# Fewer and longer runs of small products on TensorE, in a delta-rule attention block with a feed-forward part

## The chip, the cores and the metric

The kernel runs on one core of one Trainium2 chip. The metric is the device time of one execution in microseconds (us). The engines are named as in the profile: PE is TensorE (PEld its weight loads), DVE is VectorE, ACT is ScalarE, POOL is GpSimd, SP is SyncE.

## The reference

The input is `hidden_states` of shape [2, 4096, 512] in float32. It is normalized per token (`xn`), and the output is the input plus two branches of `xn`:

```python
q, k = hidden @ Wq, hidden @ Wk            # 16 heads of 32; both divided by their length
v = silu(hidden @ Wv); beta = sigmoid(hidden @ Wb)
# per head, token by token:
v_pred = S^T k_t
delta  = (v_t - v_pred) * beta_t
S      = S + k_t delta^T
o_t    = S^T q_t
attn   = (o * rsqrt(mean(o*o) + eps) * o_norm_weight) @ Wo
ffn    = (silu(xn @ gate_w8 * gate_scale) * (xn @ up_w8 * up_scale)) @ down_w8 * down_scale
out    = x + attn + ffn
```

The feed-forward weights (512 to 1536 and back) are first rounded to float8_e4m3.

## The kernel before, in words

The sequence is cut into 16 turns of 256 tokens of each of the two batches, 512 tokens a turn. In each turn the recurrence over 32 tokens at a time is put into matrix form. There are 64 heads-and-pieces on each quarter of 32 partitions (four heads lie on the four quarters), in eight groups of eight.

PE's program of a turn is written out by hand, and every step of it waits on semaphores of the engines that feed it:

- **Projections** (`project`, 13 jobs of 12 matmuls of 128x512, job 4 of 8): queries, keys, values and beta, each into one of the four banks `D`. Keys are jobs 0, 2, 5, 7, queries 1, 3, 6, 8, beta 4, values 9 to 12. ACT copies keys and queries into `kq` (`evacuate_k`, `evacuate_q`), and a job may write its bank once the job four earlier has been read.
- **Products of keys with keys and queries** (`gram(g)`, groups 0 to 7): 64 float32 products on 32x32 tiles each, into the four banks `T`. Groups 4 to 7 use the banks of 0 to 3 again, after DVE has read them (`read_grams(0)`, `mask_products(0)`). They stand between the projections.
- **Output projection** of the turn before (`project_out`, 4 jobs of 12) and the first 20 of 24 **feed-forward halves** (`gate_up(half)`, 8 matmuls each). Meanwhile DVE inverts the triangular matrices by row elimination (`row_products`, `off_rows`, 31 pairs), and between the rows it reads values (`v_to_tokens`), adds the output (`add_out`) and multiplies gate and up (`fuse_tile`). At the end it transposes the inverse in two halves (`t_transposed`).
- **Products with the inverse** (groups 0 to 7, 64 small products each, line 525): groups 0 to 3 wait for the first transposed half, groups 4 to 7 for the second and for the bank to be read by DVE (`read_w(g)`) and ACT (`copy_u(g)`). The last four feed-forward halves stand between them, half of one (4 matmuls) behind each group.
- **The chain** of eight steps: per step 64 small products with the state, six matmuls of the down projection (line 502), 64 small products that update the state, six more. It starts when all eight `read_w` and `copy_u` are done. The next turn's normalization and transposes are in it too.

The small products all go through `quads`, four 32x32 products on the four diagonal tiles, line 350 in the profile. At the head of a turn DVE runs `prepare`: it normalizes the outputs of the turn before (`o_sums`, `o_scale`, which frees ACT to make `o_hi`, then `o_low`), transposes keys (`k_to_tokens`) and beta, and reads the first products. In the opening turn `prepare_first` stands in its place, with the rounding of weights.

SP's queue carries two loads and two stores a turn; the order of its program depends on `add_out` alone.

Of the kernel before, what the change touches and what calls it, by code (L numbers as in the profile page):

```python
# [20 lines left out]
IC = INNER // P  # L21
# [5 lines left out]
PROJECTIONS = 13  # L27
# [20 lines left out]
LOW_BEFORE, LATE_HALVES = 8, 4  # L48
# [13 lines left out]
def gate_up_job(half):  # L62

    return JOB_GU + half


def bank_of(job):

    return job % 4 if job < JOB_DN + 3 else JOB_DN % 4
# [24 lines left out]
def delta_block_kernel(nc: bass.Bass, x: bass.AP, wq: bass.AP, wk: bass.AP, wv: bass.AP, wb: bass.AP,  # L94
# [11 lines left out]
    with ctx:  # L106
# [238 lines left out]
        def _(pe):  # L345
# [36 lines left out]
            def all_spans(it=0):  # L382
                for turn in range(TURNS):
# [33 lines left out]
                    def project(job, first=0, end=12):  # L417
                        bank = bank_of(job) if first else take(job)
                        group = (4, 0, 5, 1, 12, 6, 2, 7, 3, 8, 9, 10, 11)[job]
                        cols = slice(group * P, (group + 1) * P)  # L420
                        parts = ((w_hi, xt_hi), (w_hi, xt_lo), (w_lo, xt_hi))[:2 if job == JOB_B else 3]
                        products = [(k, w, xp) for k in range(KT_) for w, xp in parts]
                        for n in range(first, min(end, len(products))):
                            k, w, xp = products[n]
                            last = nc.tensor.matmul(D[bank][:, :], w[:, k, cols], xp[:, k, :],  # L425
                                                    start=n == 0, stop=n == len(products) - 1)
                        if n == len(products) - 1:
                            last.then_inc(dense_done, 1 + TILES if opening and job == JOB_V[MS - 1] else 1)

                    def gate_up(half, first=0, end=KT_):  # L430
                        bank = bank_of(gate_up_job(half)) if first else take(gate_up_job(half))
                        ic, side = divmod(half, 2)
                        c = side * INNER + ic * P
                        for k in range(first, end):
                            nc.tensor.matmul(D[bank][:, :], wgu[:, k, c:c + P], xt_hi[:, k, :], start=k == 0, stop=False)  # L435
                            last = nc.tensor.matmul(D[bank][:, :], wgu[:, k, c:c + P], xt_lo[:, k, :],  # L436
                                                    start=False, stop=k == KT_ - 1)
                        if end == KT_:
                            last.then_inc(dense_done, 1)

                    def gram(g):

                        pe.wait_ge(kwide_ready, since(MS, g // 2 + 1))
                        pe.wait_ge(qwide_ready, since(MS, g // 2 + 1))

                        if g < 4:
                            pe.wait_ge(o_ready, since(STEPS))
                        else:
                            pe.wait_ge(m_ready, since(2, 1))
                            pe.wait_ge(p_ready, since(2, 1))  # L450
                        pe.nop(nofuse=True)
                        for n in range(8):
                            both = kq_flat.rearrange("p (n t) -> p n t", t=2 * CHUNK)[:, 8 * g + n, :]
                            last = quads(T[g % 4][:, 64 * n:64 * n + 64], both[:, 0:CHUNK], both)
                        last.then_inc(tiled_done, 1)
# [2 lines left out]
                    pe.wait_ge(xt_lo_ready, since(TILES, TILES))  # L458
                    for job in range(5):
                        project(job)  # L460
                    gram(0)
                    gram(1)
                    project(5)
                    gram(2)
                    gram(3)
                    project(6)
                    project(7)
                    project(8)
                    gram(4)
                    gram(5)  # L470
                    project(9, end=5)
                    gram(6)
                    gram(7)
                    project(9, first=5)
                    for job in range(10, PROJECTIONS):
                        project(job)

                    if opening:
# [36 lines left out]
                    for g in range(8):  # L515
                        pe.wait_ge(tt_ready, since(2, g // 4 + 1))
                        if g < 4:
                            pe.wait_ge(m_ready, since(2, 2))
                            pe.wait_ge(p_ready, since(2, 2))
                        else:  # L520
                            pe.wait_ge(u_ready, since(8, g - 3))
                        pe.nop(nofuse=True)
                        for n in range(8):
                            pc = 8 * g + n
                            last = quads(T[g % 4][:, 64 * n:64 * n + 64], tt[:, pc // 32, :, pc % 32], kpv[:, 1:3, pc * DH:(pc + 1) * DH])
                        last.then_inc(tiled_done, 1)
                        gate_up(2 * IC - LATE_HALVES + g // 2, 2 * (g % 2), 2 * (g % 2) + 2)

                    def transpose_next(j):

# [4 lines left out]
                    for c in range(STEPS):  # L535
# [25 lines left out]
                        fill(fill_at(c, 1))  # L561

            all_spans()


# [6 lines left out]
        def _(act):  # L572
# [21 lines left out]
            def all_spans(it=0):  # L594
                for turn in range(TURNS):
# [13 lines left out]
                    def evacuate_k(m):  # L609
                        full(("job", JOB_K[m]))  # L610
                        bank = bank_of(JOB_K[m])
                        nc.scalar.activation(kq[:, m * BC:(m + 1) * BC, 0, :], D[bank][:, :].rearrange("p (n t) -> p n t", t=CHUNK),
                                             ACT.Copy).then_inc(kwide_ready, 1)

                    def evacuate_q(m):
                        full(("job", JOB_Q[m]))
                        bank = bank_of(JOB_Q[m])
                        nc.scalar.activation(kq[:, m * BC:(m + 1) * BC, 1, :], D[bank][:, :].rearrange("p (n t) -> p n t", t=CHUNK),
                                             ACT.Copy).then_inc(qwide_ready, 1)
# [9 lines left out]
                    evacuate_q(0)  # L629
                    evacuate_k(1)  # L630
                    evacuate_q(1)
                    evacuate_k(2)
                    if not opening:
                        act.wait_ge(on_ready, since(1))
                        nc.scalar.activation(o_hi, o_normed.rearrange("p (m n) -> p m n", m=MS), ACT.Copy).then_inc(ohi_ready, 1)
                    def beta_tanh():

                        act.wait_ge(b_summed, since(1, 1))
                        nc.scalar.activation(tb[:, :, :], tb[:, :, :], ACT.Tanh, scale=w_inv[:, 3:4]).then_inc(tb_ready, 1)

                    if not opening:
                        beta_tanh()
                    evacuate_q(2)
                    evacuate_k(3)
                    evacuate_q(3)
# [191 lines left out]
        def _(dve):  # L837
# [129 lines left out]
            def all_spans(it=0):  # L967
                for turn in range(TURNS):
# [25 lines left out]
                    def k_to_tokens(m):  # L994
                        dve.wait_ge(kwide_ready, since(MS, m + 1))
                        nc.vector.transpose(kt[:, m * BC:(m + 1) * BC, :], kq[:, m * BC:(m + 1) * BC, 0, :]).then_inc(kt_ready, 1)
# [63 lines left out]
                    def times_beta(s):  # L1060

                        dve.wait_ge(beta_ready, since(2, s + 1))
                        solved[0] = step(nc.vector.tensor_tensor(m_prob[:, s], m_prob[:, s],
                                                                 beta_t[:, s].unsqueeze(1).to_broadcast([P, CHUNK, CHUNK]), ALU.mult))
# [8 lines left out]
                    def prepare():  # L1073

                        o_sums(it, turn, after, step)
                        k_to_tokens(0)
                        k_to_tokens(1)
                        o_scale(it, turn, after, step)
                        b_to_tokens()
                        k_to_tokens(2)  # L1080
                        read_grams(0)
                        mask_products(0)
                        o_low()
                        beta_to_problems()
                        beta_over_k(0)
                        times_beta(0)
                        k_to_tokens(3)
                        set_diagonal(0)

# [36 lines left out]
                    def low_part(ic):  # L1126
                        dve.wait_ge(fhi_ready, since(IC, ic + 1))
                        nc.vector.tensor_tensor(f_lo[:, ic, :], fuse[:, ic % FUSE_RING, :], f_hi[:, ic, :],
                                                ALU.subtract).then_inc(flo_ready, 1)
# [89 lines left out]
                    low_part(8)  # L1219
                    read_w(1)  # L1220
                    low_part(9)
                    read_w(2)
                    read_statistics(0)
                    read_w(3)
                    fuse_tile(10)
                    read_w(4)
                    read_statistics(1)
                    read_w(5)
                    aggregate(0)
                    low_part(10)  # L1230
                    read_w(6)
                    aggregate(1)
# [106 lines left out]
```

## Time and profile before

| what | value |
|---|---|
| time, median of 3 runs | 2445.73 us (2445.45 to 2448.61) |
| profiled execution, its own time | 2442.38 us |
| its span, first to last instruction | 2440.6 us |
| PE busy | 95% of the span, 40944 matmuls |
| DVE busy | 74% |
| ACT busy | 35% |
| POOL busy | 11% |
| mean granted clock of TensorE | 0.992 |
| one steady turn, start to start | about 144.7 us |

PE is busy nearly all the time, so idle time of the others costs nothing unless PE waits for it. "Issue" is time in which an engine waited for nothing that the profile shows; a wait for a semaphore whose signal can't be paired can stand under that name too.

### The profile page before, as it was taken

The numbers are of one execution on the slowest core, as the hardware profiler recorded it, in microseconds if no ns is written. First come the engines' busy times: TensorE is split into PE (matmuls) and PEld (weight loads), VectorE is DVE, ScalarE is ACT, GpSimd is POOL, SyncE is SP. The second block draws the span as 40 slices with busy tenths as digits, with TensorE's granted clock in tenths as the row PEclk, the third lists the DMA queues.
The fourth block names the chain that finished last, engine by engine and source line by source line (L and its number), as shares of the span: only waits on it lengthen the run. The fifth ranks groups of instructions, "written<-read, shape, count | busy, mean of one in ns | idle before, by whom it ended". The sixth has DMA issues, their size and how long they took to land.

```text
span 2440.6 us, 90080 instructions
## 1 busy us (share of the span) xinstructions
PE 2314.6 (95%) x40944; PEld 1259.3 (52%) x40944; DVE 1817.7 (74%) x3210; ACT 861.2 (35%) x2069; POOL 275.0 (11%) x521
## 2 busy tenths in 40 slices
PE   1869999999999999999999999999999999999996
PEld 0435555554655545455554555555465554545553
DVE  7985866869677695867769586686967769586785
ACT  2353432524234252423425243242423425242341
POOL 3011002010010101001010110201001010100100
PEclk9989999999999999999999999999999999999999
DMA  6100100100010010100001010010101001010000
GB/s 216 48 1 4 36 3 3 36 3 36 4 36 3 3 36 3 36 3 12 27 3 36 3 36 3 3 36 3 36 4 36 3 3 36 3 36 3 11 28 19
DMA packets 27163, 54.30 MB, mean 22 GB/s; under 512 B 5152, under 2 KB 5152, under 8 KB 26784
## 3 DMA queue, kind: packets, MB, share of 16 engines
q1 hardware_dynamic: 26784, 48.55, 5.7%
q8 instruction: 323, 5.29, 0.9%
q14 instruction: 56, 0.46, 0.1%
HBM read 31.76 MB, written 16.78 MB: 20 GB/s over the span
## 4 chain that ended last, share of the span: by engine, by line
PE 93%; DVE 4%; issue 1%; SPq 1%; DMA 0%; POOL 0%; ACT 0%; POOLq 0%; DVEq 0%
PE T L350 22%; PE D L425 21%; PE D L502 15%; PE D L435 14%; PE D L436 13%; PE D L366 7%; PE D L355 1%; DMA ds_row<-in_L_ffn_down_scale_dram 0%; DVE wd L267 0%; DVE wgu L267 0%; DVE w_lo L921 0%; DVE outer_v L1145 0%; DVE at L1152 0%; SPq L300 0%; SPq L295 0%
## 5 line engine op out<-in xcount | busy, mean ns | idle before, releaser
L435 PE MATMUL D<-xt_hi,wgu 128*128 128x512 f16 x1536 | 586.3, 382 | 18.5 <-ACT sg L674 12.1
L436 PE MATMUL D<-xt_lo,wgu 128*128 128x512 f16 x1536 | 584.7, 381 | 0.0
L425 PE MATMUL D<-xt_hi,w_hi 128*128 128x512 f16 x832 | 317.1, 381 | 38.5 <-DVE wo_lo L925 38.5
L425 PE MATMUL D<-xt_lo,w_hi 128*128 128x512 f16 x832 | 316.5, 380 | 0.0
L502 PE MATMUL D<-wd,f_hi 128*128 128x512 bf16 x768 | 293.6, 382 | 0.3 <-issue 0.3
L425 PE MATMUL D<-xt_hi,w_lo 128*128 128x512 f16 x768 | 292.3, 381 | 0.0
L502 PE MATMUL D<-wd,f_lo 128*128 128x512 bf16 x768 | 291.1, 379 | 0.0
L1152 DVE TENSOR_TENSOR at<-at,outer_v 128x62 f32<-128x62 f32 (+15 forms) x496 | 262.4, 529 | 12.8
L1145 DVE TENSOR_TENSOR outer_v<-mt,at 128x62 f32<-128x62 f32 (+15 forms) x496 | 260.7, 526 | 11.7
L435 PEld LDWEIGHTS D<-xt_hi,wgu 128*128 128x128 f16 x1536 | 150.5, 98 | 195.7 <-ACT sg L674 12.6
L436 PEld LDWEIGHTS D<-xt_lo,wgu 128*128 128x128 f16 x1536 | 150.9, 98 | 167.4 <-issue 2.8
L664 ACT ACTIVATE kpv<-kpv,rk 128x32 f32<-128x32 f32 x1024 | 230.9, 306 | 11.0 <-POOL rk L813 9.6
L674 ACT ACTIVATE sg<-D,gs 128x512 f32<-128x512 f32 x192 | 131.8, 687 | 174.1 <-PE D L436 171.8
L668 ACT ACTIVATE f_hi<-fuse 128x512 f16<-128x512 f32 x192 | 120.6, 628 | 167.2 <-DVE fuse L1138 166.9
L350 PEld LDWEIGHTS T<-kpv,mt 32*32 32x32 f32 x8192 | 131.0, 134 | 72.6 <-issue 72.6
L350 PE MATMUL T<-kpv,mt 32*32 32x64 f32 x8192 | 148.2, 219 | 17.5 <-issue 17.5
L1264 DVE STREAM_TRANSPOSE outer_p<-T 128x256 f32<-128x256 f32 x128 | 57.6, 450 | 137.8 <-PE T L350 137.8
L1246 DVE STREAM_TRANSPOSE outer_v<-T 128x256 f32<-128x256 f32 x128 | 57.6, 450 | 131.7 <-PE T L350 131.7
L350 PEld LDWEIGHTS T<-kq,state 32*32 32x32 f32 x8192 | 121.4, 105 | 61.8 <-issue 61.5
L829 POOL TENSOR_TENSOR xs<-xs,fuse 128x512 f32<-128x512 f32 x64 | 81.1, 1267 | 639.5 <-DVE fuse L1240 639.5
L719 ACT ACTIVATE qt<-T 128x256 f32<-128x256 f32 x128 | 49.1, 383 | 291.3 <-DVE outer_p L1264 291.3
L425 PEld LDWEIGHTS D<-xt_hi,w_hi 128*128 128x128 f16 x832 | 81.5, 98 | 134.5 <-DVE wo_lo L925 38.9
(169 smaller groups left out, 3207.4 us busy)
## 6 DMA issues: line engine op xcount, KB each, us to landing
xs<-_attn_hidden_states_dram SPq DMA_DIRECT2D x34, 512.0 KB, 3.4
out_dram<-xs SPq DMA_DIRECT2D x32, 512.0 KB, 3.1
f_hi<-in_L_ffn_down_w_dram SPq DMA_DIRECT2D x2, 768.0 KB, 6.8
f_lo<-in_L_ffn_down_w_dram SPq DMA_DIRECT2D x2, 768.0 KB, 8.3
qt<-in_L_ffn_gate_w_dram SPq DMA_DIRECT2D x2, 768.0 KB, 4.3
kpv<-in_L_ffn_up_w_dram SPq DMA_DIRECT2D x2, 768.0 KB, 4.3
qt<-in_L_attn_Wq_dram SPq DMA_DIRECT2D x1, 1024.0 KB, 10.2
kpv<-in_L_attn_Wk_dram SPq DMA_DIRECT2D x1, 1024.0 KB, 13.1
```

Of the source, the lines that this page charges most:

```text
L350: last = nc.tensor.matmul(out[s], lhs[s], rhs[s], start=start, stop=True, skip_group_check=shared)
L366: ins = nc.tensor.matmul(D[bank][:, :], o_part[:, m, j * P:(j + 1) * P], w[:, m, :], start=n == 0, stop=n == 11)
L425: last = nc.tensor.matmul(D[bank][:, :], w[:, k, cols], xp[:, k, :], start=n == 0, stop=n == len(products) - 1)
L435: nc.tensor.matmul(D[bank][:, :], wgu[:, k, c:c + P], xt_hi[:, k, :], start=k == 0, stop=False)
L436: last = nc.tensor.matmul(D[bank][:, :], wgu[:, k, c:c + P], xt_lo[:, k, :], start=False, stop=k == KT_ - 1)
L502: last = nc.tensor.matmul(D[bank][:, :], (f_hi, f_lo)[n % 2][:, ic, j * P:(j + 1) * P], wd[:, ic, :], start=n == 0, stop=n == 2 * IC - 1)
L664: return nc.scalar.activation(v_problem, v_problem, ACT.Identity, scale=rk[:, n:n + 1])
L668: nc.scalar.activation(f_hi[:, ic, :], fuse[:, ic % FUSE_RING, :], ACT.Copy).then_inc(fhi_ready, 1)
L674: nc.scalar.activation(sg[:, ic % 2, :], D[bank_of(gate_up_job(2 * ic))][:, :], ACT.Silu, scale=gs[:, ic:ic + 1]).then_inc(sg_ready, 1)
L829: nc.gpsimd.tensor_tensor(xs[:, par, j, :], xs[:, par, j, :], fuse[:, j % 2, :], ALU.add).then_inc(acc_ready, 1)
L1145: solved[0] = step(nc.vector.tensor_tensor(products(j), m_prob[:, :, j, j + 1:].unsqueeze(3).to_broadcast(shape), t_prob[:, :, j, 0:j + 1] ...
L1152: solved[0] = step(nc.vector.tensor_tensor(rest, rest, products(j), ALU.subtract))
```

## The change

In PE's program the eight groups of products of keys and queries stand in two runs of four, with four whole projections between them; before they stood in four runs of two, the last of them in the middle of job 9. The eight groups of products with the inverse stand in four runs of two, with one whole feed-forward half behind each; before each group had half of one behind it. On ACT the copy of the third key job moves behind `o_hi` and beta; on DVE its transpose moves behind `times_beta(0)`, and the statistics of the next turn's input move forward by one or two reads. The number of instructions is the same.

```diff
@@ PE
                     for job in range(5):
                         project(job)
-                    gram(0)
-                    gram(1)
-                    project(5)
-                    gram(2)
-                    gram(3)
-                    project(6)
-                    project(7)
-                    project(8)
-                    gram(4)
-                    gram(5)
-                    project(9, end=5)
-                    gram(6)
-                    gram(7)
-                    project(9, first=5)
-                    for job in range(10, PROJECTIONS):
+                    for g in range(4):
+                        gram(g)
+                    for job in range(5, 9):
+                        project(job)
+                    for g in range(4, 8):
+                        gram(g)
+                    for job in range(9, PROJECTIONS):
                         project(job)
...
                         last.then_inc(tiled_done, 1)
-                        gate_up(2 * IC - LATE_HALVES + g // 2, 2 * (g % 2), 2 * (g % 2) + 2)
+                        if g % 2:
+                            gate_up(2 * IC - LATE_HALVES + g // 2)
@@ ACT
                     evacuate_q(1)
-                    evacuate_k(2)
                     if not opening:
                         act.wait_ge(on_ready, since(1))
                         nc.scalar.activation(o_hi, ...).then_inc(ohi_ready, 1)
...
                     if not opening:
                         beta_tanh()
+                    evacuate_k(2)
                     evacuate_q(2)
@@ DVE, prepare
                         b_to_tokens()
-                        k_to_tokens(2)
                         read_grams(0)
                         mask_products(0)
                         o_low()
                         beta_to_problems()
                         beta_over_k(0)
                         times_beta(0)
+                        k_to_tokens(2)
                         k_to_tokens(3)
@@ DVE, behind the inverse
                     low_part(9)
+                    read_statistics(0)
                     read_w(2)
-                    read_statistics(0)
                     read_w(3)
+                    read_statistics(1)
                     fuse_tile(10)
                     read_w(4)
-                    read_statistics(1)
+                    aggregate(0)
                     read_w(5)
-                    aggregate(0)
                     low_part(10)
```

## Rows read from the trace of the kernel before

**Rows 1.** The page: PE's busy time, and the chain that ended last
```profile
PE 2314.6 (95%) x40944; PEld 1259.3 (52%) x40944; DVE 1817.7 (74%) x3210; ACT 861.2 (35%) x2069; POOL 275.0 (11%) x521
...
PE 93%; DVE 4%; issue 1%; SPq 1%; DMA 0%; POOL 0%; ACT 0%; POOLq 0%; DVEq 0%
```

**Rows 2.** Windows: length, busy PE, PEld, DVE, ACT, POOL, clock, DMA, GB/s
```profile
1262.00:1282.00 20.00, 20.00 (x569) 12.41 (x567) 13.30 (x17) 4.42 (x6) 1.80 (x1) 1.00 0.01 3
1282.00:1336.00 54.00, 54.00 (x251) 24.36 (x249) 52.28 (x97) 28.97 (x87) 3.92 (x13) 1.00 0.12 40
1336.00:1354.00 18.00, 16.80 (x553) 10.78 (x556) 11.65 (x25) 5.48 (x12) 1.78 (x2) 1.00 0.02 5
```

**Rows 3.** Waits of PE: us in total, times, longest
```profile
PE T L350 <- issue: 20.8, 28, 1.6
```

**Rows 4.** Timeline of PE, projections and chain: start, length, instruction, count
```profile
1257.74 0.38 PE L425 MATMUL D<-xt_hi,w_lo 128*128 128x512 f16 x1
...
1279.61 0.38 PE L425 MATMUL D<-xt_lo,w_hi 128*128 128x512 f16 x1
1279.92 2.00 PE L350 MATMUL T<-kq 32*32 32x64 f32 x128
1281.85 0.39 PE L425 MATMUL D<-xt_hi,w_lo 128*128 128x512 f16 x1
...
1285.74 0.38 PE L425 MATMUL D<-xt_hi,w_lo 128*128 128x512 f16 x1
...
1356.01 0.38 PE L502 MATMUL D<-wd,f_lo 128*128 128x512 bf16 x1
1356.32 1.10 PE L350 MATMUL T<-kpv 32*32 32x64 f32 x64
1357.35 0.39 PE L502 MATMUL D<-wd,f_hi 128*128 128x512 bf16 x1
```

**Rows 5.** Timeline of PE at the products with the inverse
```profile
1335.82 0.38 PE L436 MATMUL D<-xt_lo,wgu 128*128 128x512 f16 x1
1337.17 1.15 PE L350 MATMUL T<-kpv,mt 32*32 32x64 f32 x64 [0.98 <-issue]
...
1351.55 1.15 PE L350 MATMUL T<-kpv,mt 32*32 32x64 f32 x64
...
1353.29 0.38 PE L436 MATMUL D<-xt_lo,wgu 128*128 128x512 f16 x1
1353.90 1.09 PE L350 MATMUL T<-kq,state 32*32 32x64 f32 x64 [0.22 <-ACT kpv L679]
```

**Rows 6.** Timeline of DVE from `prepare` to the transposed inverse
```profile
1277.36 0.70 DVE L996 STREAM_TRANSPOSE kpv<-kq 128x512 f32<-128x512 f32 x1
1277.99 0.17 DVE L1027 TENSOR_TENSOR at<-sig_t,rkk_t 128x32 f32<-128x32 f32 x1
1281.98 1.25 DVE L1053 STREAM_TRANSPOSE mt<-T 128x1024 f32<-128x1024 f32 x1 [3.81 <-PE T L350]
...
1286.81 0.71 DVE L1000 STREAM_TRANSPOSE kpv<-D 128x512 f32<-128x512 f32 x1
...
1334.23 0.74 DVE L1138 SCALAR_TENSOR_TENSOR fuse<-D,usf,sg 128x512 f32<-128x512 f32 x1
...
1335.72 2.37 DVE L1162 STREAM_TRANSPOSE mt<-at 128x1024 f32<-128x1024 f32 x2
```

**Rows 7.** Timeline of ACT: a key job's copy, and the last copy_u
```profile
1258.16 0.60 ACT L612 ACTIVATE kq<-D 128x512 f32<-128x512 f32 x1 [1.99 <-PE D L425]
...
1353.26 0.38 ACT L679 ACTIVATE kpv<-T 128x256 f32<-128x256 f32 x1 [1.68 <-DVE kq L1167]
```

**Rows 8.** Timeline of PE in the opening turn
```profile
185.15 1.15 PE L350 MATMUL T<-kpv,mt 32*32 32x64 f32 x64 [1.54 <-issue]
```

**Rows 9.** Instruction fetches of the page, and a gap on PE's timeline
```profile
q8 instruction: 323, 5.29, 0.9%
...
1489.37 0.34 PE L350 MATMUL T<-kpv,mt 32*32 32x64 f32 x6 [0.43 <-issue]
```

**Rows 10.** Windows, a stretch of the opening turn; columns as in rows 2
```profile
108.50:118.70 10.20, 5.63 (x79) 3.34 (x80) 9.82 (x12) 10.17 (x11) 0.00 (x0) 0.50 0.04 4
```

## The prediction, made before the kernel was run

> **What bounds the kernel now.** I read the page first, then PE's waits, a table of stages for one steady turn (the ninth of sixteen), and last the timelines of PE, DVE and ACT there. PE is busy for 95% of the span and is 93% of the chain that ended last [rows 1]. So the time is the sum of PE's work and of its few waits; what other engines do counts only where PE waits for them. In the three stages of the turn PE is full in the first two and short by 1.2 us of 18 in the third, where the inverse is handed over [rows 2]. DVE, though, is busy for 52.28 of 54.00 us in the stage of the row elimination [rows 2]: there it is a second chain, nearly as tight as PE's. PE's waits in the steady part are two in each turn: about 0.9 to 1.0 us, shown as "issue", ahead of the first product with the inverse, and 0.22 ahead of the first product with the state; the others are rare gaps or belong to the opening and the end [rows 3, 5].
>
> The first wait is DVE's: its transposes of the inverse begin at 1335.72 and the two take 2.37, so the first ends near 1336.9, and PE starts at 1337.17 [rows 5, 6]. Without it PE would have started 0.31 behind the matmul at 1335.82, as behind any dense matmul ahead of a small run [rows 4], at 1336.13. The wait is worth 1.04 us.
>
> **What a switch costs.** Dense matmuls follow each other every 0.216 us (18 steps between 1281.85 and 1285.74) [rows 4]. From the last dense matmul to the next one, a run of 128 small products takes 2.24 us (1279.61 to 1281.85), one of 64 takes 1.34 (1356.01 to 1357.35) [rows 4]. So 64 small products cost 0.90, and of the 1.34 there remain 1.34 - 0.216 - 0.90 = 0.22, plus about 0.01 by which the first dense step is longer: 0.23 us for going from dense to small and back. For products with the inverse the period of one run and four dense matmuls is (1351.55 - 1337.17) / 7 = 2.054 us [rows 5]; less 4 x 0.216 and 0.90 that leaves 0.29. Their own pace may be a little slower than 0.90 for 64, so I take 0.28; the bounds are 0.23 and 0.29.
>
> **The change, part by part.**
> *Keys and queries.* Four runs of two become two of four: two switches fewer, 0.46 us. The last run also loses what stood ahead of it: five of the twelve matmuls of project(9), 5 x 0.216 = 1.08 us, now follow. The last of these products is therefore ready 0.46 + 1.08 = 1.54 us earlier in the turn. DVE had been idle for 3.81 us waiting for it [rows 6], so read_grams(1) and the elimination move up too, if DVE's earlier work is done. It is: in the new order the products of groups 0 to 3 end before project(5) rather than after it, and the last thing DVE needs, k_to_tokens(3), gets its data from job 7. Behind job 7 PE still has project(8), 2.59 us, and four groups, 3.6; less 0.42 until ACT starts and 0.60 of its copy [rows 4, 7] that is 5.2 us ahead, for two DVE operations of 0.70 and 0.17 [rows 6]. Moving k_to_tokens(2) and evacuate_k(2) costs nothing: both engines are idle around them, and the copy o_hi, which o_low waits for, is now ahead of job 5's evacuation, which couldn't start before project(5) ended anyway. If that cover were gone, each would cost up to 0.7 us.
>
> But DVE can't move by the whole 1.54. Its second value transpose needs job 10. That job's last matmul starts at 1285.74 and its data can be read 0.42 later, as ACT started at 1258.16 behind the matmul at 1257.74 [rows 4, 7]: at 1286.16. DVE came at 1286.81 [rows 6], 0.65 late. Now PE's job 10 moves up by 0.46 only, to 1285.70, and DVE comes at 1286.81 - 1.54 = 1285.27: a new stall of 0.43 us. The elimination then ends 1.54 - 0.43 = 1.11 us earlier. The later reads of PE's banks in the elimination had more to spare. The least has fuse_tile(8), at 1334.23 [rows 6]: its job ended 16 steps of 0.216 ahead of 1335.82, so it could be read from 1332.8 on, 1.4 us earlier. Of that 0.65 goes, so there is no second stall. PE arrives 0.46 earlier. So the wait shrinks to 1.04 + 0.46 - 1.11 = 0.39, and this part gives **1.11 us** a turn: 0.46 of switches and 0.65 of wait. Bounds: 0 (if DVE gains nothing, the switches saved only lengthen the wait) and 1.50 (both whole).
>
> *Products with the inverse.* Eight runs become four: 4 x 0.28 = 1.12 us. What is late next? Group 4 needs copy_u(0), 5 needs copy_u(1), and so on. A pair now takes 2.05 + 0.90 + 0.86 = 3.83 us, so group 4 starts at 7.7 us of the stage and group 7 at 12.4; copy_u(0) to (3) are done by about 2.5, 3.4, 5.9 and 6.7, worked out from DVE's 0.45 and ACT's 0.38 behind each group's last product. The end gains: before, PE waited for copy_u(7), which started at 1353.26, 1.71 behind its group's start at 1351.55 [rows 5, 7]. The chain started at 1353.90, 0.61 behind the last dense matmul at 1353.29, where 0.31 is normal: 0.30 lost. Now eight dense matmuls, 1.73 us, stand behind group 7 in place of four, which covers copy_u(7) with about 0.6 to spare. So this part gives 1.12 + 0.30 = **1.42 us**. The reordered statistics and aggregates lie in DVE's gaps; they are ready earlier, and POOL idles until they come.
>
> *Sum.* 1.11 + 1.42 = 2.53 us in each of 15 turns, 38.0. In the opening turn the first stage is held by other waits of DVE and ACT, and the second group of four inverses starts at 185.15 behind a wait of 1.54 [rows 8]; from there two switches and the last wait go, 0.86 us. In all 38.8. The profiled execution took 2442.38 us for its span of 2440.6, so it would be 2403.6; the median of the runs shown is 3.35 above it, which gives 2445.73 - 38.8 = **2406.9 us**.
>
> **The rivals.**
> *The inverse ends no sooner.* DVE is full in that stage [rows 2], and a further read that comes late, or slower elimination steps, could hold it. Against: its start waited on PE with 3.81 us idle. Then only 15 x 1.42 + 0.86 = 22.2 are won: 2423.6.
> *The switch isn't saved.* If the 0.23 were a cost of the first and last products that waiting instructions between groups inside a run also bring, only the moved work counts: 0.65 + 0.30, 14.5 us in all, 2431.2. Against: 128 products in one run with such a wait in the middle cost only 0.90 more than 64 [rows 4].
> *The longer runs starve for instructions.* One fetched block of 5.29 MB / 323 = 16 KB serves some 127 products with their loads, and the only gaps inside small runs are named issue, as 0.43 at 1489.37 [rows 9]. A run of four uses two blocks in 3.6 us. A gap of 0.43 in each of the two runs takes 15 x 2 x 0.43 = 13 us back: 2420. Against: of PE's gaps named issue there are 28 in all [rows 3], over half of them the wait for the inverse, and 448 small runs. [...]
> *TensorE's clock falls: slower.* The opening has whole stretches at half clock, one of 10.20 us at 0.50, when PE was busy for 5.63 of it with narrow products [rows 10]. If a run of four small groups, 3.6 us with little of the array at work, did the same, a stretch in which PE is otherwise full loses half of 10.2, 5.1 us. One such stretch in each of 15 turns costs 76.5, less 38.8: 2483. It decides from eight stretches on. Against: in the stage of the eight runs, half of it such products, the clock stayed at 1.00 [rows 2]. [...]
>
> **How the numbers follow.** The forecast 0.66; the inverse no sooner 0.12; starved runs 0.07; switch not saved 0.04; some other stall in either stage, which would give 2410 to 2425, 0.04; clock 0.04; another loss or none 0.03. Measurement tells apart about 0.2%, 5 us. Faster 0.93, same 0.02, slower 0.05. The lower end is both parts whole, 15 x (1.50 + 1.42) + 0.86 = 44.7: 2401. The upper end is the rival in which the inverse ends no sooner, 2424. Between them lie some 0.85.
>
> **What would show it.** The page: PE's instructions unchanged, its waits of "issue" ahead of the inverse near 0.3 rather than 0.95; no wait on ACT L679 in the steady turns. Timeline: two runs of 256 small products of some 3.7 us, four of 128 with the next run 3.83 later; DVE's second L1000 of a turn with an idle of about 0.4 ahead of it; a turn 2.5 us shorter. Wrong if gaps stand inside the long runs, if the granted clock falls below 1.00 in steady turns, or if the wait ahead of the inverse grows to 1.5.

## The result, and the profile after

The change makes the kernel slightly slower: 2452.26 us median of 20 runs (2445.0 to 2457.17) against 2444.68 of 20 runs of the kernel before (2439.2 to 2448.61), ratio 1.0032, interval 1.0025 to 1.0038. I had forecast 2406.9, in a range of 2401 to 2424. The profiled execution took 2453.12 us, its span 2451.4 (before 2440.6).

The page after, as in [rows 1] (busy time, then the chain that ended last):

```profile
PE 2301.0 (94%) x40944; PEld 1265.2 (52%) x40944; DVE 1817.1 (74%) x3210; ACT 853.8 (35%) x2069; POOL 268.6 (11%) x521
...
PE 92%; DVE 4%; issue 2%; SPq 1%; DMA 0%; POOL 0%; ACT 0%; POOLq 0%; DVEq 0%
```

PE does the same 40944 matmuls in less busy time, and yet the span is 10.8 us longer: PE waits more. Its waits say under which name, as in [rows 3] (us in total, times, longest):

```profile
PE T L350 <- issue: 50.5, 54, 2.1
```

That is 30 us more of "issue" ahead of small products, and the wait for ACT's copy is gone from the list. The windows of the same turn, as in [rows 2], say where:

```profile
1266.00:1288.00 22.00, 19.33 (x565) 12.37 (x564) 13.76 (x16) 4.54 (x6) 1.80 (x1) 1.00 0.01 3
1288.00:1343.00 55.00, 55.00 (x258) 24.96 (x256) 52.82 (x97) 28.35 (x87) 3.93 (x13) 1.00 0.11 39
1343.00:1361.00 18.00, 16.72 (x590) 11.37 (x592) 11.23 (x25) 5.49 (x12) 1.41 (x2) 1.00 0.02 5
```

The stage of keys and queries, full before, now lacks 2.7 us of PE, at a clock of 1.00. And PE's timeline there (rows for small runs alone; a run that is broken by a gap has two rows) shows the gaps inside the runs:

```profile
1266.95 3.14 PE L350 MATMUL T<-kq 32*32 32x64 f32 x209
1271.44 0.87 PE L350 MATMUL T<-kq 32*32 32x64 f32 x47 [1.35 <-issue]
1282.71 2.44 PE L350 MATMUL T<-kq 32*32 32x64 f32 x158
1286.46 1.61 PE L350 MATMUL T<-kq 32*32 32x64 f32 x98 [1.32 <-issue]
1343.71 2.09 PE L350 MATMUL T<-kpv,mt 32*32 32x64 f32 x128 [0.29 <-issue]
1347.57 2.10 PE L350 MATMUL T<-kpv,mt 32*32 32x64 f32 x128
1351.43 2.08 PE L350 MATMUL T<-kpv,mt 32*32 32x64 f32 x128
1355.27 2.08 PE L350 MATMUL T<-kpv,mt 32*32 32x64 f32 x126
1358.34 0.27 PE L350 MATMUL T<-kpv,mt 32*32 32x64 f32 x2 [0.99 <-issue]
1360.37 1.09 PE L350 MATMUL T<-kq,state 32*32 32x64 f32 x64
```

In this turn a gap stands neither between groups (a group is 64 products) nor at a wait: 209 + 47 and 158 + 98 break in the middle of the fourth group and of the third. The 15 steady turns hold such a gap of 1 to 2 us in 26 of their 30 runs of four groups, and in a few runs of two.

The other steps of the forecast are there. The wait ahead of the inverse is 0.29 in place of 0.98 [rows 5]. Two of the runs above follow each other in 3.86 us. DVE had 6.04 us of idle time ahead of its read, and its second value transpose has the new stall (DVE's timeline, to be held against [rows 6]):

```profile
1288.11 1.25 DVE L1046 STREAM_TRANSPOSE mt<-T 128x1024 f32<-128x1024 f32 x1 [6.04 <-PE T L350]
...
1293.39 0.72 DVE L993 STREAM_TRANSPOSE kpv<-D 128x512 f32<-128x512 f32 x1 [0.35 <-PE D L425]
```

**Where the gaps stand.** I numbered PE's recorded instructions (weight loads, matmuls, semaphore events) from the first on, and took all distances of over 0.25 us between the starts of two neighbouring small products of the 15 steady turns. Beside them are the records of the queue that fetches PE's instructions, in packets of 16384 bytes, 323 of them after for 82729 recorded instructions. The table is worked out from the records of three traces that lack none of PE's:

```
kernel   gaps  with number mod 256     sum of    from the end of the last fetched
               = 192 or 193            the gaps  packet to the next product, min/median/max
before    17    17                      7.8 us   1.25 / 1.41 / 1.57
after     41    41                     51.7 us   1.20 / 1.40 / 1.73
e5        42    42                     52.0 us   1.20 / 1.40 / 1.57
```

Every gap of over 0.25 us, before and after, stands where a block of 256 instructions ends, and ends 1.4 us after the packet with the next block has landed. The seven other traces of the experiments below say the same: 233 more gaps, all with the number 192 or 193 (four of these traces lack 256 records of dense matmuls, and there the small products were counted by their weight loads). A packet of 16384 bytes for 256 instructions is 64 bytes for each. I read this as PE having run out of instructions. For the gap that ends at 1271.44 the packet began 2.7 us and ended 1.5 us ahead of the product; the block ahead of it, which ends 209 products into the run, had been used up in 1.8 us.

The theory for the experiments, an estimate from these records: PE has the block that it works through and one more at hand. With boundaries and packets numbered from the first on, 830 of the 983 packets of the three traces began behind the boundary of their own number (0.9 to 1.05 us behind it in the median), the other 153 up to 4.8 us ahead of it, none ahead of the boundary before that, and every gap ends behind the packet with the number of the boundary before it. So the fetch of a further block mostly begins when a block is done, and that block can be used some 3.3 us later (2.9 to 4.0 in the runs of four that have a gap: 0.6 to 1.6 us to the packet, 0.9 to 1.5 for it, about 1.4 behind it). A block of dense matmuls lasts 27 us (27.4 to 27.6 in the steady turns of before and after), and in e5 the 58 boundaries among dense matmuls of the steady turns are passed at the usual step of 0.216 us. One of small products alone lasts 128 x 0.014 = 1.8 us, so it leaves a gap of 1.4 to 1.9 us at its end. Rivals: an order of work that makes somebody late (waits for copies, DVE's preparation), longer runs that are slow by themselves, and the clock.

### The profile page after: what moved, and what is told of

It reads as the page before. It is cut to its first block, busy times and chain, and to the rows that moved or that the text cites. A ratio compares the mean times of both kernels' runs of the same rounds, so it can differ in the third digit from the quotient of the medians.

```text
span 2451.4 us, 90080 instructions
## 1 busy us (share of the span) xinstructions
PE 2301.0 (94%) x40944; PEld 1265.2 (52%) x40944; DVE 1817.1 (74%) x3210; ACT 853.8 (35%) x2069; POOL 268.6 (11%) x521
## 4 chain that ended last, share of the span: by engine, by line
PE 92%; DVE 4%; issue 2%; SPq 1%; DMA 0%; POOL 0%; ACT 0%; POOLq 0%; DVEq 0%
PE T L350 21%; PE D L425 21%; PE D L494 15%; PE D L435 14%; PE D L436 13%; PE D L366 7%; PE D L355 1%; DMA ds_row<-in_L_ffn_down_scale_dram 0%; DVE wd L267 0%; DVE wgu L267 0%; DVE w_lo L914 0%; DVE outer_v L1138 0%; DVE at L1145 0%; SPq L295 0%; SPq L300 0%
## 5 line engine op out<-in xcount | busy, mean ns | idle before, releaser
L1145 DVE TENSOR_TENSOR at<-at,outer_v 128x62 f32<-128x62 f32 (+15 forms) x496 | 263.2, 531 | 12.8
L350 PE MATMUL T<-kq 32*32 32x64 f32 x8192 | 129.0, 215 | 37.6 <-issue 37.6
```

The costliest lines, as they stand in the source:

```text
L350: last = nc.tensor.matmul(out[s], lhs[s], rhs[s], start=start, stop=True, skip_group_check=shared)
L1145: solved[0] = step(nc.vector.tensor_tensor(rest, rest, products(j), ALU.subtract))
```

## The experiments

All ratios are to the kernel before, run on the same chip.

### e1 and e2: each part alone

e1 is the kernel before with the part of the inverse alone:

```diff
-                        gate_up(2 * IC - LATE_HALVES + g // 2, 2 * (g % 2), 2 * (g % 2) + 2)
+                        if g % 2:
+                            gate_up(2 * IC - LATE_HALVES + g // 2)
```

with the moved statistics of DVE. e2 has the part of keys and queries alone, with the moved copy and transpose:

```diff
-                    gram(0)
-                    gram(1)
-                    project(5)
-                    gram(2)
...
+                    for g in range(4):
+                        gram(g)
+                    for job in range(5, 9):
+                        project(job)
+                    for g in range(4, 8):
+                        gram(g)
```

> The kernel before with the inverse part of the change alone: four runs of two groups, a whole feed-forward half behind each, and DVE's statistics moved. Theory (instruction blocks): PE's program is fetched in blocks of 256 instructions of which only the next one is on its way, and PE stops where a block of nearly only small products is used up in 1.8 us, before the next is there some 3.3 us after the last change of blocks. A run of two groups is 258 instructions, so it holds a whole block only where a block begins within a dozen instructions of the run's start: gaps in some four turns of fifteen, about 5 us in all. The switches and the last wait give 22 us: 17 us faster than before, ratio 0.993. Rival (the longer runs of products with the inverse are slow by themselves, by waits for copies): no gain or a loss, ratio 1.000 or more, with a gap in every turn at the same group.

> The kernel before with the keys-and-queries part alone: two runs of four groups, and the moved copy and transpose. Theory (instruction blocks): each run of 520 instructions holds at least one whole block, so each has a gap of 1.2 to 2 us in every turn, some 45 us in 15 turns, against 1.11 x 15 = 17 us won: about 25 us slower, ratio 1.010. Rival (order of the work, a wait of DVE's preparation or of the copies): the loss would stand in front of groups, not inside them, and DVE's first read of groups 4 to 7 would find its own work late; here it should find 4 us or more of idle time. Rival (clock): granted clock below 1.00 in steady turns, gaps absent.

e1: 2437.51 us, ratio 0.9955 (0.9942 to 0.9968). e2: 2467.57 us, ratio 1.0076 (1.0063 to 1.0089). So the first part wins 9 to 11 us and the second loses 19 to 21; together they give the small loss of the whole. The expectation had the signs and the order (17 won, 25 lost), and both parts were 4 to 8 us off. e2's timeline has the same picture in the same places, at the same number of products into the run as the whole change, with 5.78 us of idle time for DVE ahead of its read of groups 4 to 7, so DVE's own work isn't late:

```profile
1275.07 3.14 PE L350 MATMUL T<-kq 32*32 32x64 f32 x209
1279.38 0.87 PE L350 MATMUL T<-kq 32*32 32x64 f32 x47 [1.16 <-issue]
1290.64 2.50 PE L350 MATMUL T<-kq 32*32 32x64 f32 x158
1294.13 1.61 PE L350 MATMUL T<-kq 32*32 32x64 f32 x98 [0.98 <-issue]
```

e1 has a gap of over 0.25 us inside a run of two in four of 60 runs, two to four products ahead of its end, where a block began with the run:

```profile
1478.93 2.09 PE L350 MATMUL T<-kpv,mt 32*32 32x64 f32 x128 [0.78 <-issue]
1482.89 2.08 PE L350 MATMUL T<-kpv,mt 32*32 32x64 f32 x126
1486.61 0.27 PE L350 MATMUL T<-kpv,mt 32*32 32x64 f32 x2 [1.64 <-issue]
1488.64 2.13 PE L350 MATMUL T<-kpv,mt 32*32 32x64 f32 x128
```

These four come to 5.6 us, as expected. What I had left out are the small ones: distances of over 0.13 us between neighbouring small products, less 0.035 us each, came to 20 us in all, against 9.5 in the kernel before. More than half of them, of 0.2 to 0.9, lie in the chain of eight steps, though its program is that of before.

### e3 and e4: the same work, the blocks in two places

A turn of PE's program has 5156 instructions, 36 more than 20 blocks, so the boundaries wander by 36 from turn to turn. To hold them still, e3 adds to e1 waits that are always fulfilled, each one instruction:

```diff
+            for _ in range(10):
+                pe.wait_ge(consts, 2)
+                pe.nop(nofuse=True)
             pe.wait_ge(proj_ready, 5)
...
                     for half in range(2 * IC - LATE_HALVES):
                         gate_up(half)
+                        for _ in range(11):
+                            pe.wait_ge(consts, 2)
+                            pe.nop(nofuse=True)
```

e4 is e3 with 122 in place of 10.

> The kernel of e1 with 220 waits that are always fulfilled added to PE's program in each turn, 11 behind each of the first 20 feed-forward halves, and 10 ahead of the first turn. Each turn is then 5376 = 21 x 256 instructions, so that the block boundaries fall at the same places in each turn, 76 to 190 instructions into each small run outside the chain, away from the starts. Theory (instruction blocks): no gap of over 0.4 us in any steady turn; about 5 to 8 us faster than e1, 22 to 27 faster than before, ratio 0.990, if waits between dense matmuls cost nothing. Rival (gaps come at random or from other engines): as many gaps as e1, and the same time or longer by the added instructions.

> As e3, and only the number of fulfilled waits ahead of the first turn differs: 122 in place of 10. Work, order and instructions of every turn are the same. Now a block begins exactly with the first run of products with the inverse. Theory (instruction blocks): one gap of 1.2 to 1.6 us near the end of that first run in each of 15 turns, some 20 us slower than e3, ratio to before about 0.998. Rival (anything that lies in the work or its order): the same time as e3 within 0.1%.

e3: 2424.74 us, ratio 0.9916 (0.9903 to 0.9929). e4: 2466.0 us, ratio 1.0084 (1.0068 to 1.01). The two differ in the number of waits ahead of the first turn, in a place where PE is idle for 38 us anyway, and in nothing else, and by 41 us. e3 is 13 us faster than e1 (5 to 8 were expected) though it issues 3530 instructions more, and its longest distance between two small products inside a run is 0.59 us. PE's timeline of the same turn in e3:

```profile
1038.01 2.09 PE L350 MATMUL T<-kpv,mt 32*32 32x64 f32 x128 [0.93 <-issue]
1041.86 2.13 PE L350 MATMUL T<-kpv,mt 32*32 32x64 f32 x128
1045.76 2.08 PE L350 MATMUL T<-kpv,mt 32*32 32x64 f32 x128
1049.60 2.08 PE L350 MATMUL T<-kpv,mt 32*32 32x64 f32 x128
1053.44 1.10 PE L350 MATMUL T<-kq,state 32*32 32x64 f32 x64
```

and in e4:

```profile
1050.69 2.08 PE L350 MATMUL T<-kpv,mt 32*32 32x64 f32 x127 [0.95 <-issue]
1054.41 0.21 PE L350 MATMUL T<-kpv,mt 32*32 32x64 f32 x1 [1.64 <-issue]
1056.39 2.13 PE L350 MATMUL T<-kpv,mt 32*32 32x64 f32 x128
```

The gap stands where it was forecast, in each of the 15 turns, and is 1.6 to 2.1 us from start to start, more than the 1.4 of the theory's arithmetic. The size of the whole was off by a factor of two: some 20 us were expected, 41 were measured. In the profiled executions the gaps over 0.13 us come to 43.5 us in e4 and 7.4 in e3, 36 of the 44 us between their spans; the boundaries behind the first run fall badly in other places too. Part of the rest is the clock: in two turns, right behind the two longest gaps of the steady turns (2.13 us), the granted clock was 0.50 for 3.4 us while PE did dense matmuls, one every 0.43 us (columns as in [rows 2]):

```profile
1201.30:1204.70 3.40, 3.40 (x9) 1.04 (x8) 2.22 (x4) 0.38 (x1) 0.00 (x0) 0.50 0.02 5
```

The rivals that look to the work or its order are out.

### e5, e6, e7: the runs of four, and the kernel before, with the blocks held still

The same waits added to the changed kernel (e5 with 20 ahead of the first turn, e6 with 200) and to the kernel before (e7, with 10).

> The changed kernel with the 220 fulfilled waits of e3 in each turn, and 20 ahead of the first, so that block boundaries stand still: 180 and 76 instructions into the two runs of four groups, 48 to 102 into the runs with the inverse. Theory (instruction blocks): a run of 518 instructions still holds one whole block wherever the boundary lies, so one gap of 1.4 to 1.9 us in each of the two runs of every turn, none in the runs with the inverse: about 48 us of gaps, 3 to 8 us faster than the changed kernel, ratio to before 1.001. Rival (a good place of the blocks cures the change as it cured e1): no gaps, ratio 0.982.

> As e5, with 200 waits ahead of the first turn in place of 20: now a block begins with the first run of four groups, so that run holds two whole blocks and has two gaps, one near its middle and one near its end, each turn; the other run still one. Theory (instruction blocks): 15 x 1.7 = 26 us slower than e5, ratio to before about 1.011. Rival (a gap belongs to the long run as such, at most one in each): the same time as e5.

> The kernel before, unchanged in its order, with the same 220 waits in each turn and 10 ahead of the first. Theory (instruction blocks): its few gaps in small runs (9.5 us in all in the profiled execution) go partly, those in the chain of eight steps stay: 2 to 6 us faster, ratio 0.998. The difference to e3 is then what the inverse part of the change is worth where no block is in the way: 15 x 1.42 + 0.86 = 22 us by the prediction's sum. Rival (e3 gained from the added waits, not from the change): e7 as fast as e3, ratio 0.991.

e5: 2447.59 us, ratio 1.0002 (0.9992 to 1.0012). e6: 2462.51, ratio 1.0063 (1.005 to 1.0075). e7: 2443.1, ratio 0.9979 (0.997 to 0.9988).

In e5 the first boundary lies 89 products into the first run of four and 38 into the second. Both runs keep their gap in each of the 15 turns (30 gaps of over 0.9 us), and the runs with the inverse have none:

```profile
536.87 3.32 PE L350 MATMUL T<-kq 32*32 32x64 f32 x215
541.83 0.77 PE L350 MATMUL T<-kq 32*32 32x64 f32 x41 [1.64 <-issue]
552.99 2.54 PE L350 MATMUL T<-kq 32*32 32x64 f32 x164
556.56 1.53 PE L350 MATMUL T<-kq 32*32 32x64 f32 x92 [1.03 <-issue]
```

So these two places don't cure a run of four. It doesn't follow that none does. In the kernel after, where the boundaries wander, four of the 30 runs of four have no gap, as this one:

```profile
408.18 3.79 PE L350 MATMUL T<-kq 32*32 32x64 f32 x256
```

They are the four whose first boundary lies 10 to 14 products into the run; in the 26 others it lies 28 or more in. e2 has the same four. In all eight the packet of the block that begins at the second boundary started 1.4 to 2.4 us ahead of the run's first product, while dense matmuls were still at work. The rival of e5 is therefore refuted only for the places that were tried. Counted from the start of its run, the boundary in the second run of a turn lies 51 products ahead of that in the first, so waits added elsewhere can put at most one of them there; no run puts waits between the two, and whether the whole change would then win is not shown.

e6 went against my expectation: the first run has one gap, not two. It stands at the second boundary, three products ahead of the end; at the first, near product 127, there is none:

```profile
539.30 3.77 PE L350 MATMUL T<-kq 32*32 32x64 f32 x253
544.43 0.30 PE L350 MATMUL T<-kq 32*32 32x64 f32 x3 [1.36 <-issue]
555.13 3.03 PE L350 MATMUL T<-kq 32*32 32x64 f32 x201
559.70 0.98 PE L350 MATMUL T<-kq 32*32 32x64 f32 x55 [1.55 <-issue]
```

The packet for the block that begins there started 2.8 us ahead of the run, twelve dense matmuls before its first product. My reading is that the fetch hangs on where PE's sequencer is, and among dense matmuls that is ahead of the array: in e6's trace the first of the eleven waits behind a feed-forward half is recorded 3.65 us (median; 2.4 to 5.3) ahead of the start of the matmul that stands just before it. That reading fits the four runs without a gap, and e4, where PE stood at the wait for the inverse with the boundary right behind it: there the packet began 1.0 to 1.6 us behind the run's first product in each of the 15 turns, and the first boundary cost the full gap of 1.6 to 2.1 us. No run was made for this reading alone. e6 is 15 us slower than e5, not 26; its gaps come to 60 against 52 us, and the other half of the difference I have not located.

e7 shows that the waits by themselves are not what made e3 fast. From e7 to e3 the ratio falls from 0.9979 to 0.9916, 15 us, for 22 expected; in the two traces the 14 turns from the first product with the inverse of turn 2 to that of turn 16 take 2031.2 and 2011.0 us, 1.44 us a turn, which is the forecast's 1.42. The medians come from two chips, and I leave the difference at 15 to 20.

### e8: one operation of DVE moved

```diff
-FUSE_AT = {29: 0, 33: 1, 36: 2, 39: 3, 42: 4, 46: 5, 49: 6, 54: 7, 59: 8}
+FUSE_AT = {29: 0, 33: 1, 36: 2, 39: 3, 42: 4, 46: 5, 49: 6, 54: 7}
...
                     t_transposed(0)
+                    fuse_tile(8)
                     t_transposed(1)
```

> e3 with one of DVE's operations moved: fuse_tile(8), with the low part that goes before it, stands behind the first transpose of the inverse in place of ahead of the last rows. It takes 1.3 us off the path from the products of keys and queries to the first half of the inverse. If PE's wait ahead of the products with the inverse is DVE's elimination and nothing else (1.04 us a turn, as the prediction had it), it goes wholly: 15 x 1.04 = 16 us faster than e3, ratio to before 0.985. Rival (the wait is PE's own, a drain ahead of the first products): no gain, 0.991.

2413.59 us, ratio 0.9862 (0.9846 to 0.9879): the fastest, faster than both kernels of the case. The wait is gone in all 15 turns, the runs with the inverse begin without an idle mark:

```profile
1034.39 2.15 PE L350 MATMUL T<-kpv,mt 32*32 32x64 f32 x128
1038.31 2.10 PE L350 MATMUL T<-kpv,mt 32*32 32x64 f32 x128
```

and PE's waits fall from 19.2 us of issue in e3 to

```profile
PE T L350 <- issue: 10.3, 19, 3.2
```

The gain is smaller than the 16 us expected: 11 us between the medians, of two chips. In the traces the same 14 turns take 2003.9 us against 2011.0 in e3, 7.1 us. Some 5 us of the difference are small gaps, which came to 12.8 us against 7.4; the rest isn't located.

## Why the prediction was wrong, point by point

- **A switch costs 0.23 to 0.28 us, six go per turn: right.** Two runs with the inverse follow each other in 3.86 us, forecast 3.83. From the first of them to the chain e3 takes 15.43 us where before took 16.73 [rows 5]: 1.30 won, forecast 1.42.
- **The wait for copy_u(7) goes: right**, it is off the list.
- **The elimination ends 1.11 us earlier, with a new stall of 0.43 at job 10: right.** The stall reads 0.35, the wait ahead of the inverse 0.29 idle, where the forecast's 0.39 from start to start comes to 0.33 idle on that scale. e8 shows that the wait was DVE's. (The forecast's 3.83 for a pair adds up to 3.81 from the terms given with it; nothing hangs on the 0.02.)
- **Runs of four are as fast as two runs of two: wrong, and this is the step that failed.** The sum took 0.90 us for each 64 products whatever the length of the run. The mechanism stood among the rivals, "the longer runs starve for instructions", at 0.07 and with 0.43 us a run. Both were too low. The price came from one gap of before, 0.43 idle [rows 9], which is 0.65 from start to start; the gaps in the runs of four are 1.2 to 2.3 on that scale. And what spoke against it says nothing of a run of four: that few of 448 small runs had a gap. The longest of them were 128 products, with their weight loads 256 instructions, just one block, so they hold a whole block of nothing else only if it begins with them. A run of 256 products holds one always, and had a gap in 26 of 30. The row had the numbers for this: 16 KB for 127 products, and 3.6 us for two such blocks.
- **Sum.** In the profiled executions the gaps in the 15 steady turns (over 0.13 us, less 0.035 each) come to 52.9 us after and 9.5 before, 43.4 more, against 38.8 won by the forecast: 4.6 of the 10.8 us. The inverse part won 0.12 less a turn, 1.8. In the opening turn the granted clock was at half for 3.4 us, behind an idle time of 2.04 us of PE, amid the products with the inverse:

```profile
184.70:188.10 3.40, 3.40 (x91) 2.40 (x83) 2.43 (x7) 1.74 (x5) 0.70 (x1) 0.50 0.02 5
```

  (columns as in [rows 2]). The kernel before and e3 have 1.00 there, behind idle times of 1.54 and 1.97, but e1 has 0.50 for 3.4 us behind 1.94, so the length of the idle time alone doesn't tell which. From the first product with the inverse to the chain that turn took 19.07 us after and 17.51 in e3, some 1.6 more. Ahead of that the profiled execution of after was 1.3 us early, not late: both kernels do their first projections at half speed, a matmul every 0.43 us, before for 14 of them and after for 9. So 10.8 - 4.6 - 1.8 - 1.6 + 1.3 = 4.1 us are not placed.
- **The clock: as a cause of the loss the rival falls.** It is 1.00 in all three stages of the turn above, runs of four included, and none of the 41 gaps of after, up to 2.27 us, is followed by a lower one. It can follow: it did twice in e4 (1.92 us idle each) and once in e2, where the clock was 0.50 for 3.4 us shortly behind a gap in a run of four (1.69 us idle).

## What to carry to other kernels

Count instructions, not only time, in any stretch of short work on PE (the other engines were not tried): each 256 of its instructions here needed some 3.3 us (2.9 to 4.0) or they waited for the fetch, so a run of tiny matmuls longer than a block lost 1.2 to 2.3 us where the saved switch brought 0.23 to 0.28, unless the block boundary fell just behind the run's start (10 to 14 products into it). A little dense work inside each block (in e3 eight matmuls of 0.216 us behind each run of 128 products with the inverse) hides most of the fetch: no distance inside a run of e3 is over 0.59 us. Where the count per loop turn is no multiple of 256 the boundaries wander (here by 36 instructions a turn), so that an edit anywhere earlier in the program can move the time, as 112 more waits did by 1.7% (e3, e4). A gap named issue inside a run of the same instruction is to be looked at by its position in the program before its size is taken as small.

## What the runs showed of the hardware

- PE's instructions come in packets of 16384 bytes, 256 instructions (323 packets after for 82729 recorded instructions); all 17 gaps before, 41 after and 42 in e5 stand at one of two neighbouring numbers mod 256, as do the 233 of the other seven traces, and the next product starts 1.4 us (1.2 to 1.7) after the packet landed.
- 122 fulfilled waits in place of 10 in a stretch ahead of the first turn where PE is idle for 38 us changed the time by 41 us, 1.7% (e3, e4), with the same work in each turn.
- 220 fulfilled waits a turn between dense matmuls cost nothing that could be measured: e7 has them and is faster than before, ratio 0.9979.
- A block was fetched early where the boundary ahead of it lay at the start of a small run, behind dense matmuls: in e6 its packet began 2.8 us ahead of the run's first product and there was no gap; in after and e2 the same spared the four runs each whose first boundary lay 10 to 14 products in.
- The granted clock was 0.50 for 3.4 us behind an idle time of PE of 1.7 to 2.0 us in seven places (e4 twice, e2 once, the opening turns of after, e1, e5 and e6) and of 3.24 in the opening turn of e8, and stayed at 1.00 behind one of 1.97 (the opening turn of e3) and behind all gaps of after's steady turns.
